# Attention and mixture of experts on one core: score order, maxima, output copies and a shared mixture

## The reference

```python
# attention: 16 heads of 16, rotary positions; g = sigmoid(gate), one per head
mem_out = einsum('bhsd,bhde->bhse', q_feat, memory) / denom        # linear attention
attn = einsum('bhqk,bhkd->bhqd', softmax(q @ k.T / 4), v)          # full attention
combined = g * mem_out + (1.0 - g) * attn                          # the mixture of outputs
return combined @ Wo.T
# experts: 8 experts, 688 hidden units, each token goes to its 2 best by x @ router_w.T
```

## Time and profile before

| | |
|---|---|
| time, median of 3 (lowest to highest) | 416.09 us (415.69 to 418.0) |
| the profiled execution's own time | 417.04 us |
| its span | 415.1 us |
| granted TensorE clock | 0.989 |
| busy: TensorE, VectorE, ScalarE, GpSimd | 394.5, 248.3, 207.7, 133.0 us |
| attention (first to last turned score) | 56.6 to 258.9 us |

### The profile page before, as it was taken

How to read it: one execution, slowest core, us unless ns; L and a number is a source line. 1 busy time by engine, 2 the same in 40 slices (tenths; PEclk the granted TensorE clock), 3 DMA queues, 4 the chain that set the end, 5 groups by cost and what they waited for, 6 DMA issues and landing times.

```text
span 415.1 us, 6935 instructions
## 1 busy us (share of the span) xinstructions
PE 394.5 (95%) x2383; PEld 228.6 (55%) x2384; DVE 248.3 (60%) x504; ACT 207.7 (50%) x397; POOL 133.0 (32%) x129
## 2 busy tenths in 40 slices
PE   8999899999999999899999999999999999999992
PEld 3465462232223222432422233799989998997991
DVE  7878978878877797689889710377233232221310
ACT  4479465767767767557566798421211212121120
POOL 7349786120403105011035240215633121412322
PEclk9999989999999999999999999999999999999997
DMA  7335032194561907703014189521544122321342
GB/s 241 112 108 88 10 61 56 33 234 127 162 220 51 319 10 250 243 14 124 2 46 143 53 295 332 158 76 50 186 82 65 25 40 33 46 36 29 39 115 25
DMA packets 22812, 45.05 MB, mean 109 GB/s; under 512 B 4464, under 2 KB 15472, under 8 KB 21936
## 3 DMA queue, kind: packets, MB, share of 16 engines
q0 software_dynamic: 9280, 30.41, 26.2%
q1 hardware_dynamic: 13116, 14.00, 12.6%
q10 hardware_dynamic: 388, 0.27, 0.2%
HBM read 23.76 MB, written 15.59 MB: 95 GB/s over the span
## 4 chain that ended last, share of the span: by engine, by line
PE 69%; DVE 18%; DMA 3%; issue 3%; ACT 2%; POOL 2%; SPq 1%; DVEq 0%; POOLq 0%; ACTq 0%
PE psum L1469 66%; DVE mem L1173 11%; POOL xg_d L758 2%; ACT mem L984 1%; DMA mem<-x 1%; DMA mem<-xg_d 1%; DVE mem L1118 1%; PE psum L1619 1%; PE psum L1768 1%; DMA xg_d<-mem 1%; PE psum L1645 1%; DVE mem L1128 0%; DVE mem L1238 0%; PE psum L1663 0%; DVE mem L1209 0%
## 5 line engine op out<-in xcount | busy, mean ns | idle before, releaser
L1469 PE MATMUL psum<-mem 128*32 128x512 f32 (+13 forms) x2251 | 383.6, 402 | 11.1 <-DVE mem L1173 4.4
L1469 PEld LDWEIGHTS psum<-mem 128*128 128x128 f32 (+7 forms) x2251 | 215.2, 145 | 166.9 <-issue 64.4
L1173 DVE TENSOR_REDUCE mem<-psum 128x1 f32<-128x1024 f32 x128 | 151.5, 1217 | 29.6 <-PE psum L1469 29.0
L984 ACT ACTIVATE mem<-psum 128x512 f32<-128x512 f32 x256 | 137.4, 606 | 61.3 <-PE psum L1469 59.4
L1008 ACT ACTIVATE mem<-psum 128x384 f32<-128x384 f32 (+3 forms) x32 | 15.1, 472 | 72.5 <-PE psum L1469 72.5
L782 POOL DMA_INDIRECT sum_d<-mem x17 | 26.7, 1569 | 68.5 <-ACT mem L1016 42.0
L739 POOL DMA_DIRECT2D mem<-gate_up x21 | 15.3, 732 | 101.5 <-DMA mem<-mem 101.5
L1338 DVE COPY mem<-mem 128x3 f32<-128x3 f32 x18 | 3.1, 174 | 54.5 <-PE psum L1768 54.5
L1351 DVE TENSOR_TENSOR mem<-mem,psum 128x384 f32<-128x384 f32 (+3 forms) x32 | 16.8, 527 | 30.6 <-ACT mem L1011 28.6
L1016 ACT ACTIVATE mem<-psum,mem 128x256 f32<-128x256 f32 x18 | 8.5, 474 | 40.8 <-PE psum L1469 38.4
L758 POOL DMA_INDIRECT xg_d<-mem x16 | 15.7, 983 | 7.3 <-issue 4.5
(11 more groups left out here) (134 smaller groups left out, 194.7 us busy)
## 6 DMA issues: line engine op xcount, KB each, us to landing
xg_d<-mem POOLq DMA_DIRECT2D x8, 1036.0 KB, 11.9
mem<-gate_up POOLq DMA_DIRECT2D x8, 688.0 KB, 4.4
mem<-gate_up POOLq DMA_DIRECT2D x8, 624.0 KB, 6.9
mem<-down POOLq DMA_DIRECT2D x4, 1024.0 KB, 9.1
mem<-mem SPq DMA_DIRECT2D x54, 64.0 KB, 2.7
mem<-mem SPq DMA_DIRECT2D x18, 128.0 KB, 4.3
mem<-xg_d SPq DMA_DIRECT2D x16, 129.5 KB, 2.2
mem<-x SPq DMA_DIRECT2D x4, 256.0 KB, 4.3
```

The source lines that it names most:

```text
L984: nc.scalar.activation(prob[:, t % 8], psum[:, score_bank(n, t)], ACT.Exp, scale=HD ** -0.5).then_inc(exp_ready, 1)
L1173: V.tensor_reduce(mx[:, par, k:k + 1], banks(2 * (k % 2), 2), AX.X, ALU.max).then_inc(max_ready, 1)
L1469: return nc.tensor.matmul(*a, **k)
```

## The change

Five edits, all inside the attention. (1) In units 1 to 6 the cast of the maxima stays at s == 31, the subtract moves to s == 1 and the transpose to s == 3 of the next unit; SP issues the keys of quad 3 ahead of unit 1's rows. (2) TensorE issues the look-ahead scores in another order: none in steps t % 4 == 1, two in a row in t % 4 == 3. (3) `osb_copy` is at r == 1, but for the tail. (4) In units 0 to 3 VectorE does the reciprocal at r == 10 and the large product at r == 12; GpSimd does the small product and the addition. TensorE's return to bank 7 no longer waits for the addition where t > 32. (5) The steps of `POST`, `SIDE` and `RETURNS` for unit 4 and the norms of unit 5 move 2 to 4 steps back, and the loop's jump moves from r == 10 to r == 12 (`PEEL` 13).

```diff
-PEEL = 11
+PEEL = 13
...
-        RETURNS = {NQ: 25, NQ + 1: STEPS, NQ + 2: RETURN}
+        RETURNS = {NQ: 29, NQ + 1: STEPS, NQ + 2: RETURN}
...
         POST = {NQ * STEPS + n: w for n, w in {
-            12: (0, "combT", 0), 13: (0, "copy", 0), 14: (0, "combT", 1), 15: (0, "copy", 1),
-            16: (0, "wo", 0), 19: (0, "wo", 1),
+            15: (0, "combT", 0), 16: (0, "copy", 0), 17: (0, "combT", 1), 18: (0, "copy", 1),
+            19: (0, "wo", 0), 22: (0, "wo", 1),
...
         SIDE = {NQ * STEPS + n: w for n, w in {
-            17: ("add", 0), 19: ("stats", 0), 21: ("add", 1), 23: ("stats", 1), 27: ("stats", 2), 29: ("stats", 3),
-            31: ("spread", 0), 33: ("norm", 0), 35: ("norm", 1), 37: ("norm", 2), 39: ("norm", 3),
-            41: ("norm", 4), 43: ("norm", 5), 45: ("norm", 6), 47: ("norm", 7),
+            21: ("add", 0), 23: ("stats", 0), 25: ("add", 1), 27: ("stats", 1), 29: ("stats", 2), 31: ("stats", 3),
+            33: ("spread", 0), 35: ("norm", 0), 37: ("norm", 1), 39: ("norm", 2), 41: ("norm", 3),
+            43: ("norm", 4), 45: ("norm", 5), 47: ("norm", 6), 49: ("norm", 7),
...
@@ SP
             stacks(2)
+
+            k_stack(3)
             max_rows(1, 1)
             sp.wait_ge(lo_ready[2], 1)
-            stacks(3)
+            first_queries(3)
...
@@ GpSimd, called behind stage_v in units 0 to 3
+            def mix(u):
+
+                pool.wait_ge(oT_read, 4 * u + 1)
+                nc.gpsimd.tensor_tensor(den_g, den_r, shares(u), ALU.mult).then_inc(oT_read, 1)
+                pool.wait_ge(lin_scaled, 2)
+                pool.wait_ge(oT_read, 4 * u + 3)
+                nc.gpsimd.tensor_tensor(mixed(u), mixed(u), linear(u, 0), ALU.add).then_inc(oT_read, 1)
...
@@ ScalarE
-                if r == 3 and t > 3:
+                if r == (3 if isinstance(n, int) and n >= TAIL else 1) and t > 3:
                     osb_copy(u - 1, (t // STEPS - 1) % 2)
...
@@ VectorE
                 if s == STEPS - 1:
                     dve.wait_ge(max_ready, pair + 1)
                     V.tensor_copy(mhl[:, 0], mx[:, par]).then_inc(mhl_ready, 1)
+                    if isinstance(u, int) and u in (0, UNITS - 1):
+                        low_maxima(u, par)
+                        turn_maxima(u)
+                elif s in (1, 3) and not (isinstance(u, int) and u < 2):
+                    if s == 1:
+                        low_maxima(u - 1, 1 - par)
+                    else:
+                        turn_maxima(u - 1)
...
-                if r == TURN + 1 and t > TURN + 1:
-                    unit = u - 1
-                    mix(unit, (u + 3) % NQ, 0 if not isinstance(n, int) or unit < NQ else 1)
+                if r in (TURN + 1, TURN + 3) and t > STEPS:
+                    if isinstance(u, int) and u > NQ:
+                        if r == TURN + 1:
+                            mix(u - 1, (u + 3) % NQ, 1)
+                    elif r == TURN + 1:
+                        mix_sums(u - 1)
+                    else:
+                        mix_outputs(u - 1, (u + 3) % NQ)
...
@@ TensorE
-                        pe.wait_ge(oT_read, 4 * u)
+                        pe.wait_ge(oT_read, 4 * u - (t > STEPS))
...
-                if isinstance(n, int) and n < 2 * (LEAD - FIRST):
+                if isinstance(n, int) and n < 2 * (LEAD - FIRST) - 1:
                     for k in range(2 - n % 2):
                         score(i, FIRST + t + (t + 1) // 2 + k)
-                elif not (isinstance(n, int) and n + LEAD >= ALL):
-                    score(i, t + LEAD)
+                else:
+                    for k in {3: (0, 1), 0: (1,), 1: ()}.get(t % 4, (0,)):
+                        if not (isinstance(n, int) and n + k + LEAD >= ALL):
+                            score(i, t + k + LEAD)
```

More of the change, by code:

```diff
@@ L388, in block_kernel, with shares, mixed, linear @@
             STEPS + 33: ("base", 0)}.items()}
+        def shares(qd):
+            return omg.rearrange("p (q j) -> p q j", q=NQ)[:, qd].unsqueeze(1).to_broadcast([P, 4, 4])
+        def mixed(qd):
+            return comb.rearrange("p n (q c) -> p q n c", q=NQ)[:, qd]
+        def linear(qd, hf):
+            return lin[:, 4 * hf:4 * hf + 4].rearrange("p n (q c) -> p q n c", q=NQ)[:, qd]
         def shared(t):
@@ L530, in stacks, with first_queries @@
                 k_stack(qd)
+                first_queries(qd)
+            def first_queries(qd):
                 sp.wait_ge(k_in, 16 * GROUPS * qd)
@@ L1177, in score_side, with low_maxima, turn_maxima @@
                     V.tensor_copy(mhl[:, 0], mx[:, par]).then_inc(mhl_ready, 1)
-                    dve.wait_ge(mhl_ready, 2 * u + 1)
-                    V.tensor_tensor(mhl[:, 1], mx[:, par], mhl[:, 0], ALU.subtract).then_inc(mhl_ready, 1)
-                    dve.wait_ge(mhl_ready, 2 * u + 2)
-                    dve.wait_ge(mrow_in, 64 * u)
-                    V.transpose(mT, mhl.rearrange("p s k -> p (s k)")).then_inc(mT_ready, 1)
+                    if isinstance(u, int) and u in (0, UNITS - 1):
[6 more added lines that the diff above has]
+                        turn_maxima(u - 1)
+            def low_maxima(u, par):
+                dve.wait_ge(mhl_ready, 2 * u + 1)
+                V.tensor_tensor(mhl[:, 1], mx[:, par], mhl[:, 0], ALU.subtract).then_inc(mhl_ready, 1)
+            def turn_maxima(u):
+                dve.wait_ge(mhl_ready, 2 * u + 2)
+                dve.wait_ge(mrow_in, 64 * u)
+                V.transpose(mT, mhl.rearrange("p s k -> p (s k)")).then_inc(mT_ready, 1)
             def mask_state():
@@ L1197, in _, with mix_sums, mix_outputs @@
                     mask_state()
+            out_bank = psum[:, 7].rearrange("p (b j c) -> p b j c", b=4, j=4)
+            def mix_sums(u):
+                dve.wait_ge(oT_ps, u + 1)
+                V.reciprocal(den_r, out_bank[:, :, :, HD]).then_inc(oT_read, 1)
+            def mix_outputs(u, qd):
+                dve.wait_ge(oT_read, 4 * u + 2)
+                V.tensor_tensor(mixed(qd).rearrange("p n (j c) -> p n j c", c=HD), out_bank[:, :, :, 0:HD],
+                                den_g.unsqueeze(3).to_broadcast([P, 4, 4, HD]), ALU.mult).then_inc(oT_read, 1)
             def mix(u, qd, hf):
[L1201 to L1203 removed]
+                mix_sums(u)
                 dve.wait_ge(oT_read, 4 * u + 1)
[L1205 to L1210 removed]
+                V.tensor_tensor(den_g, den_r, shares(qd), ALU.mult).then_inc(oT_read, 1)
+                mix_outputs(u, qd)
                 dve.wait_ge(oT_read, 4 * u + 3)
                 dve.wait_ge(lin_scaled, 2)
[L1213 to L1214 removed]
+                V.tensor_tensor(mixed(qd), mixed(qd), linear(qd, hf), ALU.add).then_inc(oT_read, 1)
             def add_x(hf, n):
```

12 lines of the change are left out of this document (1 added, 11 removed).

## The result

| | before | after |
|---|---|---|
| time, median (lowest to highest) | 416.6 us (415.69 to 418.0, 6 runs) | 412.55 us (411.42 to 412.82, 6 runs) |
| ratio to before, 95% interval | | 0.9874 (0.9835 to 0.9913) |
| the profiled execution, its span | 417.04, 415.1 us | 411.7, 409.6 us |
| first to last turned score | 202.25 us | 196.81 us |

Faster, by 5.2 us by the ratio (3.6 to 6.9 by its interval) and by 4.05 us by the two medians, where 5.1 had been added up. The median is 1.5 above the forecast of 411.0: 0.5 of it is that the runs of before stood at 416.6, and not at the 416.09 from which I had subtracted, and 1.05 is that the medians lie 4.05 apart and not 5.1. It is inside the range of 408.8 to 415.0.

A forecast was written before the change was run, and what follows sets the result against it. TensorE was taken to set the attention's pace, with waits behind VectorE and ScalarE to be won. Unit terms of 0.3 to 1.1 us summed to 5.1, from a median of 416.09 to 411.0, range 408.8 to 415.0.

The forecast's parts named there:

- What bounds: Attention: TensorE sets the pace, VectorE and ScalarE can hold it up; waits of 1.4 to 2.0 us per loop unit.
- Part 1, the chain: Maxima at r = 19: subtract and transpose deferred, only the cast stays; wins 0.38 us per unit less 0.1 for the cast.
- Part 2, the order: Two look-ahead scores in a row: 0.4 us a unit won at two-bank waits, 0.2 stays, less VectorE slack.
- slack of 0.17: VectorE's reduces in the new order: 0.17 us to spare per four-step period, against 0.39 in the old.
- The term for unit 4 (0.6): Unit 4's sum: 0.6 us won there, beside 0.24 and 0.7, before losses are subtracted.
- Part 3, the copy: Output copy moved from r = 3 to r = 1: product at r = 5 stops waiting, 0.24 us in units 1 to 6.
- Part 4, the mixture: Mixture shared with GpSimd: wins 0.65 us in unit 2, 0.14 in others; large product loses 0.2, 0.4 with the jump.
- Part 5, queues and later steps: Rows of maxima just fit or miss by 0 to 0.2 us; unit 4's transposes stop waiting, second projection 0.3 to 0.4 late.
- Rows late: Rival: every unit's first turned score waits for the rows of maxima, 1 to 3 us lost, 413.0; chance 0.13.
- GpSimd late: Rival: GpSimd's mixture operations take 2.5 us or more, VectorE waits at r = 12, 414.5 us; chance 0.05.
- VectorE the bound: Rival: two scores in a row stretch the reduce cycle past 2.85 us; at 3.05 the time is 421; chance 0.09.
- Nothing moves: Rival: waits taken away come back at the next operation on the same path, 415.5 us; chance 0.10.

The follow-up runs named there:

- order_back: The changed kernel with the look-ahead scores in the old order, one in each step; 417.82 us, ratio to before 0.9927.
- jump_14: The changed kernel with the loop's jump one step later (14 steps written out in place of 13); 410.98 us, ratio to before 0.985.
- mix_back: The changed kernel with all four mixture operations on VectorE at r = 10 again in units 1 to 4; 416.8 us, ratio to before 0.9904.
- mix_5: jump_14 with unit 4's mixture shared with GpSimd too and unit 5's transposes, copies and ranking 2 steps back; 411.98 us, ratio to before 0.9867.
- extra_ab: The changed kernel with one added VectorE operation every fourth step, between the reduce at r = 3 mod 4 and the next reduce; 419.6 us, one run.

## Why the prediction was right, point by point

**What bounds.** Right. TensorE sets the pace in units 1 to 3, and what it lost there were S waiting for a reduce, T waiting for ScalarE, and the product behind the copy. After has units of 23.63 and 23.66 against a floor of 23.3.

**Part 1, the chain.** The mechanism was right, 0.38 was right for the old order, and the cast costs 0.08 at most where I gave it 0.1. What was missing is that the 0.38 is no fixed price: in the new order it is 0.61. I had subtracted every part from before, one at a time, with before's slack of 0.39, while the order had already brought it down. For the whole change this does no harm, since the chain is gone from it; but it makes the worth of chain and mixture next to the order too small, and that of the order, had it been made alone, far too good.

**Part 2, the order.** The 0.4 a unit came (0.34, 0.48, 0.31), and so did the 0.2 that stay. The slack of 0.17 measures 0.14. The term for unit 4 (0.6) is 0.54: the waits ahead of T there fall from 0.70 to 0.16. In unit 0 the 0.3 of the chain came (`order_back` has 27.30 there, 0.27 below before), but the score that the order moves there from unit 6 takes 0.22 of it back, which I had not counted. I had also not counted it in unit 6, whose 0.5 is right with its help.

**Part 3, the copy.** 0.24 in each unit was right for 1 to 4 and wrong for 5 and 6. This could have been seen ahead: in the trace of before the product at r = 5 is 0.24 late in units 1 to 4 and not late in units 5 and 6.

**Part 4, the mixture.** The sizes were off, all on the good side but one. GpSimd's 16 elements take 0.22 us, where I had 0.8, chosen because the nearest row was of the same engine. That is just below the lower end of my bounds; the end at 0.26, VectorE's time for such an operation, was the better guide: with so few elements the length of the row of 512 says little. Its addition took 0.72 (0.75 forecast). The large product stands between A and B as forecast and moves B by 0.35 (A 116.07, B 117.55), but the S behind it is only 0.06 late in units 1 and 3, where I had 0.2, for the T of r = 12 and 13 are 0.1 late in the same period and give that much back as slack. The jump cost about what I had said (0.5 against 0.4) for another reason. I had put it on VectorE, between A and B, but the row is TensorE's: at r = 12 TensorE has just waited for ScalarE, so nothing seems to be queued behind which its jump could hide, while at r = 10, and at r = 13 in `jump_14`, it costs nothing. And the wait of bank 7 for the addition (0.2) was there to 0.06, only hidden behind the jump until `jump_14` took that away. Two prices in the same place did not add up.

GpSimd takes 0.72 for 256 elements where VectorE takes 0.41 for the large product of that size, a ratio of 1.75. The Trainium skill ("GPSIMD Engine Reference", Engine selection) advises VectorE for such work, GpSimd being about two times slower. The rate is near what the page has, and still `mix_back` is half a microsecond slower in units 1, 3 and 4: on VectorE the operations stand where A and B are; behind GpSimd's, all that waited was the one T into bank 7, by 0.26 in unit 2 of `jump_14` and of `mix_5`.

**Part 5, queues and later steps.** The rows of maxima land 4.29 behind the transpose, as in the earlier trace rows, and just fit, with 0.3 to 0.45 to spare and not none. In unit 4 the transposes of the mixture no longer wait (in the earlier trace rows they did). TensorE alone, units 4 and 5 of after:

```profile
170.99 4.18 PE L1515 MATMUL psum<-mem 128*128 128x256 f32 x21 [0.29 <-ACT mem L991]
175.51 8.30 PE L1515 MATMUL psum<-mem 128*128 128x256 f32 x42 [0.33 <-DVE mem L1261]
...
190.50 2.04 PE L1515 MATMUL psum<-mem 96*128 96x512 bf16 x12 [0.46 <-DVE mem L1197]
...
195.12 0.63 PE L1710 MATMUL psum<-mem 128*128 128x128 f32 x4 [0.47 <-DVE mem L1255]
...
206.37 3.02 PE L1515 MATMUL psum<-mem 96*128 96x512 bf16 x16 [0.48 <-DVE mem L1197]
210.13 1.03 PE L1515 MATMUL psum<-mem 96*128 96x512 bf16 x11 [0.75 <-DVE mem L1197]
```

The second projection (175.51) waits for its addition on VectorE, as forecast. Unit 4 won 0.85 and not 0.4. Counted by how late TensorE's rows are, the copy gave 0.24 and the order 0.54, the stats took back 0.5 (0.19 and 0.31), all close to the forecast; but the transposes and projections went from 1.55 to 0.95 late, so 0.6 was won where I had 0.7 less 0.4, and the large product cost nothing where I had 0.2.

Unit 5 is where the prediction was most wrong, 0.58 for 1.1. It says itself that "VectorE is nearly the bound, with the smaller slack", and then adds up the terms of a unit that TensorE bounds. VectorE is busy 26.6 of 29.3 us there, and every wait of the last four rows is for it. In before the same unit waited less for reduces (TensorE alone):

```profile
212.71 3.22 PE L1469 MATMUL psum<-mem 96*128 96x512 bf16 x24 [0.27 <-DVE mem L1173]
216.30 1.82 PE L1469 MATMUL psum<-mem 96*128 96x512 bf16 x11 [0.36 <-DVE mem L1173]
```

Over the unit the order took the waits ahead of T from 1.3 to 0.1 us, more than the 0.8 forecast, but what S and transposes wait for VectorE rose from 2.3 to 3.0, where I had it fall by 0.1 (0.5 less 0.4). The 0.24 of the copy was not there to win.

**The rivals.** *Rows late* and *GpSimd late*: neither, the one by 0.3 us, the other by 1.45. *VectorE the bound*: in units 1 to 3 not, with 0.14 of slack. `extra_ab`, which overdraws it, shows that the mechanism is real. Its single run took 419.6, no less than the 419.1 of before beside it. The price that I had put on the rival was too high, though: since a wait gives slack back to the next period, an overdraft is not lost in full in each of 50 periods. *Nothing moves*: this is true of the order alone, and of unit 5 for copy and mixture, not of the whole.

## What to carry to other kernels

Price a wait by the slack that the new order leaves, not by the slack of the old one: a part that shortens one engine's path and takes slack from another's makes every operation left on that other one dearer, and parts undone one by one then add up to more than the whole (7.4 against 4.9 here). Where an engine is full up to a tenth, don't add up terms of the other engine. Small operations are free or dear by their place between the two that someone waits for: 0.34 us in each period cost 1.0 us a unit at the one place and nothing at the other. Before adding a term to a unit, look whether the wait is in that unit's rows. And put a loop's jump where the engine that sets the pace has a long row of work queued, not right behind one of its waits.
